# One pass over the scores of the four-head units moves from GpSimd to ScalarE

## The reference

```python
att = einsum('bhid,bhjd->bhij', q, k) / sqrt(8)        # causal
S  = relu(att[:, 0]), first column and diagonal zero   # from head 0 alone
FF = cumsum of S, shifted down by one row
att = att - FF
keep = the 101 least FF of each row, and the diagonal  # others -inf
y  = softmax(att) @ v
out = x + y @ w_proj.T + b_proj + experts(x)
```

## Time and profile before

| what | value |
|---|---|
| runs of the kernel before | 660.14, 663.17 and 664.04 us, median 663.17 |
| the profiled execution | 660.72 us, of which the trace spans 658.8 us |
| busy share of TensorE / VectorE / GpSimd / ScalarE | 85 / 77 / 67 / 57% |
| mean granted TensorE clock | 0.967 of full speed |

### The profile page before, as it was taken

One profiled execution on the slowest core, in us unless ns is written; L12 is line 12 of the kernel. 1 busy time (PEld: TensorE's weight loads), 2 busy tenths in 40 slices (PEclk: granted clock), 3 DMA queues, 4 the chain that ended last, 5 costly groups with the idle time before them and its releaser, 6 DMA issues.

```text
span 658.8 us, 16724 instructions
## 1 busy us (share of the span) xinstructions
PE 558.0 (85%) x5431; PEld 380.9 (58%) x5431; DVE 507.2 (77%) x2173; ACT 373.7 (57%) x781; POOL 443.2 (67%) x740
## 2 busy tenths in 40 slices
PE   4647879889887998989888888989988899899994
PEld 1423545666466655656466655666566565676583
DVE  7878698757996789858997679858897689965351
ACT  3452676555765565664756555663757556455543
POOL 7518748695578856796478945797458965596451
PEclk9655999999999999999999999998999999999999
DMA  4152053135001520035000530025100450000000
GB/s 100 24 62 28 3 63 34 30 49 60 1 17 29 62 32 1 24 46 63 8 17 20 61 42 2 17 43 64 17 1 15 51 57 1 1 15 5 1 2 17
DMA packets 30070, 19.58 MB, mean 30 GB/s; under 512 B 6089, under 2 KB 29856, under 8 KB 29984
## 3 DMA queue, kind: packets, MB, share of 16 engines
q1 hardware_dynamic: 29984, 18.50, 20.9%
HBM read 3.22 MB, written 2.10 MB: 8 GB/s over the span
## 4 chain that ended last, share of the span: by engine, by line
PE 49%; DVE 19%; ACT 9%; POOL 9%; issue 8%; SPq 4%; DMA 1%; DVEq 1%; ACTq 0%; POOLq 0%
PE ps_t L900 12%; PE ps_o L919 9%; PE ps_s L887 7%; PE ps_m L832 6%; POOL ar L542 5%; DVE ar L1314 4%; SPq L405 4%; PE ps_m L844 4%; PE ps_m L828 3%; ACT pr L714 2%; ACT h L699 2%; ACT work L639 2%; POOL hsum L556 1%; PE ps_m L850 1%; ACT parts L568 1%
## 5 line engine op out<-in xcount | busy, mean ns | idle before, releaser
L542 POOL TENSOR_SCALAR ar<-ar,mx 128x512 f32<-128x512 f32 (+3 forms) x512 | 280.6, 560 | 174.7 <-DVE mx L1314 174.6
L1314 DVE CUSTOM_DVE_ANT_0 ar<-ps_s,mask 128x512 f32<-128x512 f32 (+3 forms) x512 | 230.9, 484 | 54.1 <-PE ps_s L887 52.8
L714 ACT ACTIVATE pr<-ps_t 128x512 f32<-128x512 f32 (+1 forms) x352 | 193.1, 558 | 108.7 <-PE ps_t L900 106.6
L900 PE MATMUL ps_t<-ident,ar 128*128 128x128 f32 x1280 | 202.2, 276 | 15.9 <-ACT pr L714 10.6
L900 PEld LDWEIGHTS ps_t<-ident,ar 128*128 128x128 f32 x1280 | 156.5, 142 | 54.0 <-issue 24.9
L887 PE MATMUL ps_s<-ks,qs 96*128 96x512 bf16 (+3 forms) x512 | 130.8, 308 | 17.3 <-DVE mx L1314 17.3
L919 PE MATMUL ps_o<-pr,va 128*32 128x128 f32 x2560 | 97.4, 279 | 6.0 <-ACT pr L714 5.6
L919 PEld LDWEIGHTS ps_o<-pr,va 128*32 128x32 f32 x2560 | 62.5, 110 | 45.9 <-ACT pr L714 28.6
L887 PEld LDWEIGHTS ps_s<-ks,qs 96*128 96x128 bf16 x512 | 43.3, 99 | 62.4 <-DVE mx L1314 31.1
L832 PE MATMUL ps_m<-zm,b_t 128*128 128x512 f32 x128 | 67.7, 610 | 8.4 <-ACT h L699 8.3
L699 ACT ACTIVATE h<-ps_m,bi_col 128x512 f32<-128x512 f32 x64 | 44.0, 687 | 53.8 <-PE ps_m L832 53.1
(11 more groups left out here) (220 smaller groups left out, 743.3 us busy)
## 6 DMA issues: line engine op xcount, KB each, us to landing
qs<-parts SPq DMA_DIRECT2D x42, 128.0 KB
ks<-parts SPq DMA_DIRECT2D x42, 128.0 KB
xs<-in_L_attn_x SPq DMA_DIRECT2D x8, 256.0 KB, 2.9
out<-res SPq DMA_DIRECT2D x8, 192.0 KB, 2.1
first_heads<-parts SPq DMA_DIRECT2D x72, 8.0 KB
qs<-parts SPq DMA_DIRECT2D x12, 64.0 KB
ks<-parts SPq DMA_DIRECT2D x12, 64.0 KB
out<-res SPq DMA_DIRECT2D x8, 64.0 KB, 12.9
```

The source lines that it names most:

```text
L542: nc.gpsimd.tensor_scalar(col, col, -1.0, mx[:, t % NA_RING, j:j + 1], ALU.mult, ALU.add)\
L714: nc.scalar.activation(pr[:, u % NP_RING, 0:w], ps_t[u % NT_RING][:, 0:w], ACT.Exp, scale=-1.0)\
L900: last = nc.tensor.transpose(ps_t[u % NT_RING][:, P * j:P * j + P], ar[:, u % NA_RING, P * j:P * j + P], ident[:, :])
L1314: nc.vector.tensor_tensor_reduce(out=ar[:, t % NA_RING, w * j:w * j + w], in0=ps_s[t % NS_RING][:, w * j:w * j + w], in1=mask[:, k % 2, OF ...
```

## The change

The passes `ar = mx - ar` of the four-head units (16 of 64 passes of an item, 128 in all, each 128 x 128) leave GpSimd. ScalarE does them as ACTIVATE with function Identity, scale -1 and the maximum as a bias pointer, in place. They stand two steps behind their scores, ahead of the exponential of that step. `turn` of these units waits for a semaphore of its own, `lowered`; the count of `shifted` leaves them out for the other units.

```diff
@@ GpSimd, at step t
-                            for j in range(g):
+                            for j in range(g if a else 0):
 
                                 col = ar[:, t % NA_RING, w * j:w * j + w]
                                 pool.wait_ge(masked, NH * NA * k + HEADS_TO[o] - g + j + 1)
@@ ScalarE, at step t, after the copies of other work, ahead of the exponential of unit t - LAG_T
+                        k, o = divmod(t - 2, NU)
+                        if 0 <= k < B and UNITS[o][0] == 0:
+                            act.wait_ge(masked, NH * NA * k + HEADS_TO[o])
+                            for j in range(UNITS[o][2]):
+                                col = ar[:, (t - 2) % NA_RING, P * j:P * j + P]
+                                nc.scalar.activation(col, col, ACT.Identity, scale=-1.0,
+                                                     bias=mx[:, (t - 2) % NA_RING, j:j + 1]).then_inc(lowered, 1)
                         u = t - LAG_T
@@ TensorE, turn(u)
-                        pe.wait_ge(shifted, NH * NA * k + HEADS_TO[o])
+                        if a == 0:
+                            pe.wait_ge(lowered, NH * k + HEADS_TO[o])
+                        else:
+                            pe.wait_ge(shifted, NH * (NA - 1) * k + HEADS_TO[o] - NH)
```

More of the change, by code:

```diff
@@ L315, in build @@
                  "selected", "mask_done", "h_sum", "stored", "dve_chain", "pool_chain",
-                 "act_chain", "sel", "zeroed", "zeroed_1", "w_first", "w_rows", "w_small", "b_ready"]
+                 "act_chain", "sel", "zeroed", "zeroed_1", "lowered", "w_first", "w_rows", "w_small", "b_ready"]
         s = {n: sem(n) for n in names}
@@ L326, in build @@
         dve_chain, pool_chain, act_chain, sel = s["dve_chain"], s["pool_chain"], s["act_chain"], s["sel"]
+        lowered = s["lowered"]
         zeroed, cut_set, counted, rested, parted = s["zeroed"], s["cut_set"], s["counted"], s["rested"], s["parted"]
```

## The result

The changed kernel takes 674.02 us (median of 4 runs, 671.4 to 677.85) where the kernel before takes 662.09 us in the same comparison (4 runs). The difference of the medians is +11.9 us. The ratio is 1.0183 with a 95% interval of 1.0141 to 1.0224, that is +9.3 to +14.8 us. The forecast was 675 us, +12.5.

A forecast was written before the change was run, and what follows sets the result against it. The prediction took queue order at each item's start as the bound, ScalarE running 0.30 us ahead of TensorE. 6 x 1.76 + 1.9 = 12.5 us on 660.7 gives 673.2, on the median 675.7; forecast 675 us, range 667 to 682.

The forecast's parts named there:

- The slack and the queue: Start of items 1 to 6: ScalarE's exponential has 0.30 us slack, groups take 1.2 us, each item gets 1.76 us longer.
- The price of a pass: On ScalarE: passes start 0.3 us apart, 1.2 us per group of four, taken from the Relu at line 628.
- Item 7: Last item, no DMA wait to hide the first group: weigh(1) at 592.85, not 590.94, 1.9 us late.
- Rival 1: At the next item's s0: the DMA wait of 2.35 us absorbs six of seven delays, total 665 us; chance 0.08.
- Not given back: At the next item's s0: the 1.76 us delay stays, because SyncE issues those DMAs behind the projection, itself late.
- The removal: GpSimd loses 128 passes, 45.6 us busy; counted at 0 in items 1 to 6, 0.27 us inside item 7's replay.
- VectorE's sums: Cumulative sums of 511 and 383 columns: less GpSimd work beside them returns 0 to 0.5 us an item, at most 3.
- the low end: Of the forecast sum: the only place where VectorE's possible gain of at most 3 us was counted.
- Rival 3: TensorE's clock falls after the new waits, at most 11 us on top, 687, at half the items 681; chance 0.13.
- The sum: Whole kernel: 6 x 1.76 + 1.9 = 12.5 us slower; 5 us with cheap passes, 18 or 20 with dear ones.

The follow-up runs named there:

- e1: The changed kernel with ScalarE's four passes behind the exponential and the copy to out_t of their step, not ahead; 668.1 us, 1.0099 of the kernel before.
- e2: The kernel before, GpSimd keeping its passes, with ScalarE doing four unused passes of the same size where the change put them; 673.7 us, ratio 1.0166.
- e4: The changed kernel with each group of four 128-column passes made one pass of 512 columns; 666.1 us, 1.0066 of the kernel before.
- e6: The kernel before with SyncE issuing the first_heads DMAs ahead of the store of three query tiles, not behind it; 666.4 us, ratio 1.0065.
- e3: The kernel before with the four-head units' passes done by no engine, turn waiting for VectorE's scores instead; 660.4 us, ratio 0.9972.
- e10: The kernel before with only the last piece of each item's mask made at step 6, not step 1; 659.9 us, ratio 0.9984.
- e5: The changed kernel with only units 0 and 1 on ScalarE, one step behind their scores, behind the exponential; 663.8 us, 1.0034 of the kernel before.
- e9: The kernel before with first_heads DMAs issued ahead of the store and the last mask piece at step 6, not step 1; 650.5 us, ratio 0.9846.
- e12: The changed kernel with first_heads DMAs issued ahead of the store and the last mask piece at step 6; 664.9 us, 1.0045 of the kernel before.

## Why the prediction was right

**The slack and the queue.** The step that carried the forecast was that 0.30 us of slack stand against 1.2 us of passes at three places. Forecast for item 2, and measured with the 1.10 us taken off by which s0 is later (214.31 against 213.21): `weigh(43)` 216.04, measured 216.00; `weigh(0)` 218.8, measured 218.71; `weigh(1)` 221.0, measured 220.73; the last row 225.99, measured 225.95. e1 (order), e2 (cost alone) and e4 (size) show that this is the cause. The same three waits of 0.90, 0.70 and 0.40 us stand in items 1, 2, 4, 5 and 6 (to 0.01 us), and e2 has them too (0.91, 0.70 and 0.40 us in item 4).

**The price of a pass.** Forecast 0.3 us apart and 1.2 us a group; measured 1.17. Line 628 was the right row to take it from. ScalarE's busy time grew by 34.2 us, where near 40 were forecast.

**Item 7.** Forecast 1.9 us late at `weigh(1)`. Measured from line 628 on (593.81 against 584.24, so 9.57 us off), TensorE in item 7:

```profile
596.31 0.63 PE L911 MATMUL ps_t<-ident,ar 128*128 128x128 f32 x4 [1.41 <-ACT pr L722]
...
597.87 1.08 PE L930 MATMUL ps_o<-pr,va 128*32 128x128 f32 x32
...
600.71 0.43 PE L930 MATMUL ps_o<-pr,va 128*32 128x128 f32 x8 [1.00 <-ACT out_t L731]
...
602.27 0.42 PE L930 MATMUL ps_o<-pr,va 128*32 128x128 f32 x8
```

602.27 - 9.57 = 592.70 against 590.94: 1.76 us late, 0.1 less than forecast. The path is a little another: `weigh(1)` itself does not wait; it is `weigh(0)` that is late, at 591.14, where 591.15 was forecast.

**Not given back.** Rival 1 had the next DMA wait take up the delay. At the start of item 2 that wait is 2.64 us, not shorter than the 2.35 of before; over all six it is 11.05 us after and 11.00 before. The delay goes through to SyncE, as argued. What the expectation of e6 added, that the item gets shorter by this wait once it is gone, failed: GpSimd's 15 us chain stood right behind it.

**The removal.** Counted at 0 in items 1 to 6: e3 has -1.3 us in all, right.

**VectorE's sums.** Their two instructions took 1.41 + 1.16 us in item 2 before; after, in item 2:

```profile
L1072 DVE TENSOR_TENSOR_SCAN ft<-ones,s x2: 1158/1272/1386, 222.7 to 224.0; 128x511 f32<-128x511 f32 x1, 128x383 f32<-128x383 f32 x1
```

1.39 + 1.16: nothing came back there. In items 3 to 6 a little did: from the start of the first sum to the end of the second it was 2.60 to 2.63 us before and is 2.47 after, 0.6 us in all, within the 0 to 3 that were kept for the low end. It can't be put down to the passes that left, since e2 and e10, in which GpSimd keeps them all, have 2.47 as well. The Trainium skill's rule (GPSIMD Engine Reference, section Key points: contention with VectorE instructions that read two SBUF inputs) would have given 9.5 us for the sum, the rows alone 12.5, and 11.9 was measured. The rule itself is not refuted by that, since passes of the two-head units still ran beside the sums; that the change would lift the whole difference of the earlier trace rows is.

**The clock.** Rival 3 did not decide the result: TensorE was as busy as before, 558.8 against 558.0 us. Its clock fell once between s0 of item 1 and the end of item 6 in either profiled execution, in item 5 before and in item 3 after (granted clock 0.50 and 0.68 from 291 to 295 us). The mean clock of the four runs of the changed kernel was 0.959 to 0.967, and the slowest run had the lowest clock.

**The sum.** 6 x 1.76 + 1.9 = 12.5 forecast, 11.9 measured, between bounds of 5 and 20. That it is so close is in part luck. From s0 to the next s0 the items 1 to 5 got 1.99, 1.62, 2.33, 2.39 and 0.01 us longer, not 1.76 each. The 2.33 of item 3 has the fall of the clock after the change in it, 2.39 has 0.8 us of TensorE standing still (last section), and the 0.01 has the fall before the change: item 5 took 76.10 us before, but 74.38 in e3 and 74.41 in e10, whose clock did not fall there. s0 of item 1 came 0.9 us earlier after the change, where the forecast had item 0 at 0 to 1.8 us longer. This point lies anywhere from 135.3 to 139.8 us in the 14 profiled executions, and why stays open.

## What to carry to other kernels

An engine's idle share says nothing of what a new instruction costs there: look at how long before its reader each result behind the new one is ready now. Here that slack was 0.30 us, and 1.2 us of passes ahead of it cost 0.9 us and more, in an engine that was idle 43% of the span. Look at the granted clock of a stretch before its waits are read: in item 2 of e1, e2, e4 and e5 a slow TensorE hid waits that the other items have. Of a wait that seems lost time, ask which engine stands next behind it, and move both; one alone can make a kernel slower (e6) or do nothing clear of noise (e10), where the two together gave 10 to 12 us (e9).

## What was not expected of the hardware

- A GpSimd pass takes longer beside VectorE's two-input sum: one of 128 x 256 took 482 to 485 ns from 293.0 us on (four of them, before) and 1373 ns where it overlapped the sum of 511 columns (219.0 to 221.6 us, before), while that sum varied between 1.21 and 1.55 us.
- The same wait does not always bring the same clock. In item 2, behind the wait for the DMA of 2.35 to 2.64 us, the mean granted clock from s0 to `ft` was 1.00 before, after, in e3 and in e10, and 0.87 or 0.88 in e1, e2, e4 and e5 (waits of 2.35 to 2.40 us). In e6 a wait of 1.76 us for `zm`, behind a stretch that had been busy, was followed by about 7 us at 1.2 GHz. What makes the difference stays open.
- In all 14 profiled executions TensorE once stood still with nothing to wait for, in item 4, at the same place of its program: 1.34 us before, 2.12 us after, and between 0.20 us (e6) and 2.17 us (e12) in the others. The cause stays open; it explains 0.8 us of the 2.4 by which that item got longer.
